# Low weights of the one-hot codes multiplied on GpSimd, high weights on VectorE

## The reference: four layers of a graph network

```
h = relu(layernorm(x))
g = sigmoid(h @ W_gate + b_gate);  m = g * (h @ W)
x = x + segment_sum(edge_weight[:, None] * m[dst], src)          # layer 0
h = relu(layernorm(x))
x = x + segment_sum(h[src], dst) @ W1.T + b1                       # layer 1, and so on
```

## Time and profile before

| | |
|---|---|
| median of 3 runs | 2705.81 us (2705.47 to 2713.33) |
| profiled execution, its own time | 2705.83 us |
| its span, first to last instruction | 2703.9 us |
| busy in the span: PE, DVE, ACT, POOL | 2359.7, 1605.8, 1239.3, 37.9 us |
| first and last L862 (the build) | 130.4 and 1378.8 us |

### The profile page before, as it was taken

The page is one execution under the profiler, slowest core; times in us unless marked ns, Lnnn a source line. Parts: engine busy times, 40 slices in busy tenths (PEclk is TensorE's granted clock), DMA queues, the critical chain, the costliest instruction groups (busy, mean ns, idle before and its releaser), DMA issues. The chain is left out here.

```text
span 2703.9 us, 72658 instructions
## 1 busy us (share of the span) xinstructions
PE 2359.7 (87%) x27976; PEld 2019.8 (75%) x27976; DVE 1605.8 (59%) x3701; ACT 1239.3 (46%) x2693; POOL 37.9 (1%) x46
## 2 busy tenths in 40 slices
PE   3679898998889898988974999899998999999996
PEld 2457777777777776777764888788887888878774
DVE  6679998998989898998964233333343212121114
ACT  2477776777777676777734222223222000011113
POOL 3100000000000000000000000000000000000000
PEclk9689999999999999999987999999999999999997
DMA  6289999999999999999998999989998999999994
GB/s 186 66 155 195 199 204 195 188 201 178 196 178 203 194 183 199 180 208 180 201 185 209 277 276 275 280 230 250 255 254 224 289 290 290 271 235 249 248 252 116
DMA packets 1745895, 584.13 MB, mean 216 GB/s; under 512 B 1258166, under 2 KB 1742394, under 8 KB 1745511
## 3 DMA queue, kind: packets, MB, share of 16 engines
q1 hardware_dynamic: 1742379, 572.41, 100.7%
q0 software_dynamic: 1600, 4.92, 0.6%
q10 hardware_dynamic: 1660, 3.20, 0.5%
HBM read 255.26 MB, written 89.20 MB: 127 GB/s over the span
## 5 line engine op out<-in xcount | busy, mean ns | idle before, releaser
L1155 ACT CAST stage<-ps 128x784 f16<-128x784 f32 x784 | 655.0, 835 | 134.9 <-DMA counts_by_source<-stage 96.1
L611 PE MATMUL ps<-Ha,a_pairs 128*128 128x258 f16 x4802 | 548.6, 274 | 47.0 <-ACT Ha L1200 39.2
L611 PEld LDWEIGHTS ps<-Ha,a_pairs 128*128 128x128 f16 x4802 | 470.2, 98 | 117.2 <-ACT Ha L1200 39.4
L564 PE MATMUL ps<-hot_c,hot_r 128*128 128x98 f16 x3136 | 513.4, 213 | 11.2 <-DVE hot_c L862 5.9
L565 PE MATMUL ps<-hot_c,hot_r 128*128 128x98 f16 x3136 | 507.6, 211 | 6.5 <-issue 6.5
L566 PE MATMUL ps<-hot_c,hot_r 128*128 128x98 f16 x3136 | 506.5, 211 | 0.0
L1138 ACT CAST stage<-ps 128x392 f16<-128x392 f32 x784 | 397.6, 507 | 200.6 <-PE ps L547 200.6
L539 PE MATMUL ps<-g_in,wt 128*128 128x128 f16 x2401 | 438.9, 225 | 43.3 <-DVE X L874 31.3
L540 PE MATMUL ps<-g_in,wt 128*128 128x128 f16 x2401 | 435.8, 223 | 0.0
L541 PE MATMUL ps<-g_in,wt 128*128 128x128 f16 x2401 | 435.2, 223 | 0.0
L874 DVE SCALAR_TENSOR_TENSOR X<-ps,X 128x512 f32<-128x512 f32 (+1 forms) x637 | 391.9, 653 | 17.0 <-PE ps L541 17.0
(11 more groups left out here) (198 smaller groups left out, 2106.7 us busy)
## 6 DMA issues: line engine op xcount, KB each, us to landing
a_pairs<-counts_by_source SPq DMA_DIRECT2D x75, 3136.0 KB, 14.1
counts_by_source<-stage SPq DMA_DIRECT2D x50, 1568.0 KB, 9.3
gated_parts<-G SPq DMA_DIRECT2D x7, 448.0 KB, 3.0
g_in<-gated_parts SPq DMA_DIRECT2D x98, 32.0 KB, 3.3
out_x<-X SPq DMA_DIRECT2D x6, 512.0 KB
edge_table<-tab SPq DMA_DIRECT2D x1, 2448.0 KB, 9.6
wt<-stage SPq DMA_TRANSPOSE x98, 10.9
a_turned<-counts_by_source SPq DMA_TRANSPOSE x49, 8.8
```

The lines of the kernel that those rows point to most:

```text
L564: mm(into(0), rows_, codes(0), start=v == 0, stop=True, skip_group_check=True)
L611: last = mm(ps[:, c % 2, 0:PARTS], a_slot(ph, c, i), moving[:, i], start=i == 0, stop=i == TILES - 1)
L1155: a.copy(stage[:, b, 0:2, :, u * SET_COLS:(u + 1) * SET_COLS], of).then_inc(s("hi_done"), 1)
```

## The change

VectorE's L862 multiplies by the high weights only. The low weights are multiplied by a new loop on GpSimd, which waits for the codes of the same hot (`hot_codes`, raised when L859 ends) and raises `hot_lows`, for which TensorE now waits too. The numbers and their places in SBUF are the same.

```diff
+            def low_weights(j, k, c):
+                for h in range(TILE_HOTS):
+                    hot = j * TILE_HOTS + h
+                    pool.wait_ge(s("hot_codes"), hot + 1)
+                    key = meta_w[:, bass.ds(hot * PAIRS, PAIRS), 1].unsqueeze(2).to_broadcast([P, PAIRS, WCOLS, 2])
+                    g.tensor_tensor(hot_c[:, h % 2, :, 2], hot_c[:, h % 2, :, 0], key, ALU.mult).then_inc(s("hot_lows"), 1)
+
             def layers(general):
                 if not general:
+                    pool.wait_ge(s("meta_w"), BATCHES)
+                    tiles_loop(pool, low_weights, 0)
                     return
...
                         pe.wait_ge(s("hot_ready"), j * TILE_HOTS + (h + 1))
+                        pe.wait_ge(s("hot_lows"), j * TILE_HOTS + (h + 1))
...
-                    v.tensor_tensor(hot_c[:, b, :, 1:1 + WEIGHTS], hot_c[:, b, :, 0].unsqueeze(2).to_broadcast([P, PAIRS, WEIGHTS, WCOLS, 2]),
-                                    meta_w[:, pairs].unsqueeze(3).to_broadcast([P, PAIRS, WEIGHTS, WCOLS, 2]), ALU.mult).then_inc(s("hot_ready"), 1)
+                    v.tensor_tensor(hot_c[:, b, :, 1], hot_c[:, b, :, 0], meta_w[:, pairs, 0].unsqueeze(2).to_broadcast([P, PAIRS, WCOLS, 2]), ALU.mult).then_inc(s("hot_ready"), 1)
```

## The result

The changed kernel takes 2938.85 us (median of 4 runs, 2938.25 to 2944.67), against 2708.31 for the kernel before in the same runs: a ratio of 1.0854, 95% interval 1.0831 to 1.0877. It is 230 us slower; +324 was predicted. The profiled execution is the slowest of the four, 2944.67 us with a span of 2942.7.

A forecast was written before the change was run, and what follows sets the result against it. VectorE was taken as the build's pacemaker, with the store's chain behind it; 1.46 us of delay less 0.40 saved a hot gave +317 over 46.6 tiles, +324 in all: 3030 us, range 2730 to 3230.

The forecast's parts named there:

- What bounds the kernel: In the build: VectorE sets the pace at 22.9 us a tile; waiting for the store brings it towards 25.5.
- the formula: Build tile: half of VectorE's 22.9, 0.9 of rest and the 26.5 us store chain, 25.2; shorter builds return about half.
- What the change takes away: VectorE's L862 in each hot: half the elements, its step falls from 0.88 to 0.48, saving 0.40 us.
- The exclusive wait: In the build: VectorE's two-SBUF-input instructions and GpSimd's SBUF-reading one exclude each other whole; the multiply is delayed 1.46 us.
- Who goes first: Inside a hot, after L860: GpSimd asks at 0.62, the high weights are due at 1.08, so GpSimd is served first.
- the rival in which VectorE keeps its turn: Inside a hot: high weights directly follow L860, GpSimd runs after and holds the next L859; 2734 us, chance 0.15.
- The row that the prediction decided this by: Start stage, 57.22: GpSimd waiting behind L777 went on from 57.72, not after L778, read as first to ask served first.
- The size of GpSimd's work: GpSimd's new multiply of 784 elements: two inputs read one after the other at the cast's rate, 1.63 us.
- The sum: Whole kernel: a hot 1.06 us longer, a tile 32.3 for 25.5, +317, with the first nineteen hots +324.
- GpSimd beside VectorE without a collision: In the build: the two do not exclude each other and TensorE's 20.6 us bounds; 2650 us, faster side's chance 0.09.
- a far slower GpSimd: GpSimd's new multiply at the rate of its generated elements, 4.6 us: to 4140 us; much slower cases together 0.06.
- TensorE's granted clock: In the build: 0.97 falling to its lower level in the new waits, about 3490 us; much slower cases together 0.06.

The follow-up runs named there:

- the short chain with both weights on VectorE: The kernel before without the transposes of the low weights, TensorE using the high weights' transposed tile twice: 2607.76 us (one run).
- the write-only run: Kernel before (VectorE multiplies both weights), plus GpSimd generating 196 numbers into an unread tile, with the change's waits and one more: 2703.56 us, ratio 0.9986.
- the copy: Kernel before (VectorE multiplies both weights), plus GpSimd copying the 784 codes, one SBUF input, into an unread tile: 2845.07 us (one run).
- the run with two inputs: Kernel before (VectorE multiplies both weights), plus GpSimd multiplying the low weights again into an unread tile: 3088.81 us (one run).

## Why the prediction was right, and where its sizes were off

**What bounds the kernel.** VectorE as the pacemaker, with the store's chain taking back a part, held: the short chain with both weights on VectorE came out at 2608 for the 2610 that 22.9 us and a small rest give. What the formula lets a shorter build return was too much. With the low weights left out the kernel gained 27 us and the formula said 56; its 26.5 us for the chain, read from one tile, is not a constant.

**What the change takes away.** 0.40 us a hot: shown. The multiply is 0.56 us in the run where GpSimd asks later, and giving the 0.40 back cost 150 us, where 0.40 × 373 is 149.

**The exclusive wait.** Shown from both sides. A GpSimd instruction that reads SBUF lengthens VectorE's multiply, with one input by 0.63 us and with two by 1.29; one that reads nothing does not, nor are the adds held. The page of the Trainium skill named in the prediction, "SBUF — State Buffer", section "Who interferes with whom", also says that an instruction which only writes does not contend in this way with VectorE's two-input instructions; the write-only run agrees, with L877 at 0.96. That run writes 196 elements where the copy wrote 784; an instruction that writes as many and reads none was not run. That both engines work on the same tile is not needed: in the earlier trace rows the cast and L777 read different ones.

The rows chosen for the prediction suggest that only VectorE's two-input instructions are held, and that is not so. L782 in the start stage of the kernel before has one input, in SBUF:

```profile
89.59 0.41 DVE L782 TENSOR_SCALAR pre<-pre 128x512 f32<-128x512 f32 x1
...
99.27 1.01 DVE L782 TENSOR_SCALAR pre<-pre 128x512 f32<-128x512 f32 x1
```

and GpSimd beside the second of them:

```profile
99.07 0.93 POOL L449 CAST G<-H 128x896 f16<-128x896 f32 x1 [10.48 <-ACT H L1118]
```

It takes 1.01 us instead of 0.41, so it worked from 99.87, 0.13 before the cast's end at 100.00, like the two-input instructions. The build has none of this kind, so the forecast did not suffer.

**Who goes first.** In the changed kernel GpSimd starts 0.33 us ahead of VectorE's multiply (719.14 and 719.47), and in every hot it went first; L873's durations in the 392 hots, in ns (shortest, median, longest):

```profile
L873 DVE TENSOR_TENSOR hot_c<-hot_c,meta_w x392: 1852/1855/1862, 134.8 to 1618.0; 128x784 f16<-128x784 f16 x196
```

Moved behind the multiply, GpSimd held the next L870 instead. Both fit the one that asks first; the rival in which VectorE keeps its turn would have left the multiply at 0.56 in the changed kernel. That rival's price of 2734 is close to the 2742 of the run that put this order in place, though with a hot of 3.19 us where it had 3.01, so the closeness is partly luck. The row that the prediction decided this by could not decide it: in the earlier trace rows L778 keeps its usual 0.41 us (57.77) inside GpSimd's instruction, which by the prediction's own reading worked from 57.72 to 58.66. The two did not exclude each other there, so the row shows that GpSimd waited for L777, and not who goes first when both wait. The right order was, as far as that row goes, a lucky choice; it is the experiments that show it. Whether a waiting GpSimd would go ahead of VectorE even if it asked second, no run shows.

**The size of GpSimd's work, the mis-sized term.** 1.63 us was taken, twice the cast's rate. It is 1.48 to 1.50. The delay is 1.30 instead of 1.46 a hot: the 0.15 of it that are GpSimd's own make 56 of the missing 94 us over 373 hots. The estimate from the page "GPSIMD Engine Reference", section 3.1, of the Trainium skill, 1.72, lay farther off. The copy of one input took 0.83, against the 0.82 from the cast's row.

**The sum.** A hot's builds take 2.85 us, a tile 8 × 2.85 + 6 × 1.20 = 30.0, measured 30.5 (196.49 to the last multiply's start at 1618.0, 46.6 tiles) for the 32.3 of the forecast. Of these 1.8 the builds give 1.4, 1.2 of it GpSimd's; and 0.5 us of other waits were left where I had kept 0.9, which is 19 us more. The first nineteen hots cost 4.1 us more instead of 7: the restart waits 7.05 us now and waited 15.08. The part behind the build is the same, 1324.7 us from the last multiply on and 1325.1 before; the start stage of the profiled execution was 4.4 us longer (the first L870 starts at 133.8, the first L859 at 129.3), which is not the change's doing: the same instruction starts at 132.9, 133.6 and 134.3 in the three kernels whose GpSimd has nothing to do in the build. What moves it, no run shows. The new wait for `hot_lows` cost nothing, as forecast: the profile has no wait of TensorE for GpSimd.

**The other rivals.** GpSimd beside VectorE without a collision, and a far slower GpSimd, did not happen; TensorE's granted clock was 0.99 in the build, so its new waits did not lower it.

## What to carry to other kernels

Before work goes from VectorE to GpSimd, list which VectorE instructions will run at that moment and how many of their inputs lie in SBUF. Where GpSimd reads SBUF, nearly its whole duration lands on the next one with two; one with a single input in SBUF was held too (L782), and those with one input in PSUM were not. The place where GpSimd asks counted for more here than the amount that was moved: the same work cost 230 us behind the codes and 33 behind the multiply, and three quarters of it, in the hots with adds, gained 20. A start stage that overlapped the two engines a few times was enough here to read the wait and its length before anything was built, but not the order: for that, look for a row in which both engines wait.

## What was not expected of the hardware

GpSimd's float16 multiply grew by 0.33 us from 588 to 784 elements (1.17 and 1.50, both without a wait), by an estimate from these two points 1.7 ns an element and some 0.2 fixed. The copy of 784 took 0.83, so two inputs cost less than two readings of one (1.66).

GpSimd started 0.19 us after its release in the changed kernel (L870 ends at 718.95), where the cast of the start stage took 0.06. In the run with two inputs, whose GpSimd instructions stand in a row without a loop, the start falls 0.08 behind. The changed kernel itself shows both: its first 56 hots, also in a row, have 1.88 us of GpSimd where the loop has 1.76, with the same end. So the loop makes the difference; that its address computation is the cause was not tested, and L871 hides the time.
